# GpSimd begins every second quad of gathers only when the quad before has landed

## The chip, the cores and the metric

The kernel runs on one NeuronCore of a Trainium2 chip, as one program. The metric is the device time of one execution in microseconds (us); lower is better. The engines are TensorE (PE in the profile; PEld is its weight load), VectorE (DVE), ScalarE (ACT), GpSimd (POOL) and SyncE (SP), each with its own instruction stream; they meet at semaphores. All data are fp32.

## What is computed

A block of layers on 6250 nodes with 256 features and 206250 directed edges, sorted by destination. It has three parts; the first is the one that matters here:

```python
src, dst = edge_index
norm = edge_weight * rsqrt(deg_out[src] * deg_in[dst] + EPS)
def _gcn_layer(x, W, b, src, dst, norm, n_nodes):
    xt = x @ W
    msg = xt[src] * norm[:, None]
    agg = segment_sum(msg, dst, num_segments=n_nodes)
    return relu(agg + b)
h6 = _gcn_layer(layernorm(x), W6, b6, ...)
h7 = _gcn_layer(h6, W7, b7, ...)
out = h7 @ Wp + bp
```

A linear attention over the same rows is added to it, and then comes a mixture-of-experts feed-forward layer of which two of eight experts are used, with layer norms. The two graph layers need the feature rows of all source nodes, edge by edge, twice.

## The kernel before

Edges are handled in tiles of 128. The kernel sums over edges first and multiplies by W afterwards. Each of the two graph layers is one **pass** (L = 0 and L = 1 in the code), and in each pass the edge tiles go one of two ways.

Some tiles are *gathered*: GpSimd fetches their 128 source rows from a table in HBM (`t1` in pass 0, 258 floats a row; `t2` in pass 1, 256 floats) by an indirect DMA, one row to a partition (L1960). Four tiles are a **quad** (`QT = 4`), and a quad fills one slot of a ring in SBUF (`msg`, named `ringb` in the profile) that has `RQ = 6` slots. Pass 0 has NQS[0] = 246 quads and pass 1 has 216, so 462 quads and 1848 gathers. Each slot has its own semaphore `s_g[slot]`, to which every gather adds 16 when it has landed, 64 for a quad.

The other tiles are *dense*: for them a block A of adjacency weights (128 destinations by all nodes) is built from one-hot products (L680), and TensorE multiplies it with the feature rows X (L702). In pass 0 the blocks of A are also stored to HBM, and in pass 1 most of them are loaded back by SyncE, in transfers of 1600 KB (L2031 and L2039). Before pass 1 SyncE also reloads X from `t2` in five parts of 1250 KB (L2056).

Both ways are interleaved by hand. TensorE runs through numbered steps. In step s, `sums(L, s)` first does quad s (`mm`, L654 to L665): it waits until the quad has landed (L657) and until its selection matrix `Sb` is ready, multiplies the four tiles, and increments `s_mm`, which frees the ring slot. Then, in the same in-order stream, come the builds, dense products and transposes of that step, and in pass 1 the second layer's row work. VectorE makes `Sb` four quads deep (L1219, L1234); in pass 0 it also reads one column of the gathered rows for that (L1227) and so waits for the landing too.

GpSimd's program (`pool_program`, L1897) does nothing but gathers in the two passes. For quad j it waits, once the ring is full, until TensorE has used the quad six before (L1953), and then issues four gathers (L1958 to L1961). Pass 1 begins when `t2` is stored. After pass 1 the expert layer follows (L873, L886), with 13 small operations of GpSimd (L1965) and no gather. SyncE's loads and stores run on their own queue and share the 16 DMA engines with the gathers.

Of the kernel before, what the change touches and what calls it, by code (L numbers as in the profile page):

```python
# [24 lines left out]
NQ = NG * GR  # L25
# [23 lines left out]
RQ = 6  # L49
# [125 lines left out]
def column(L, j):  # L175

    return GT * SG[L][j // GR] + QT * (j % GR)
# [92 lines left out]
def gnn_block(nc, srcT, srcR, dstT, dstR, dstO, wO, wT, x, W6, b6, W7, b7, Wp, bp, wkvT, woT, wq, bo, lng, lnb,  # L270
              Wr, br, W1, b1, W2, b2, gamma, beta, need, out):
    ctx = ExitStack()
    with ctx:
# [6 lines left out]
        def sem(name):  # L280
            return ctx.enter_context(nc.semaphore(name))
# [171 lines left out]
        s_g = [sem(f"s_g{i}") for i in range(RQ)]  # L453
# [35 lines left out]
        def loads_of(n, parity):  # L489

            return (n + 1 - parity) // 2
# [1405 lines left out]
        def pool_program(e):  # L1897
            e.iota(iof[:, :], [[1, max(HR, P)]], base=0, channel_multiplier=0,
                   allow_small_or_imprecise_dtypes=True).then_inc(s_const, 1)
            e.iota(pidx[:, :], [[0, 1]], base=0, channel_multiplier=1,  # L1900
                   allow_small_or_imprecise_dtypes=True).then_inc(s_const, 1)
            e.memset(ones[:, :], 1.0).then_inc(s_const, 1)
            e.memset(eps5[:, :], 1e-5).then_inc(s_const, 1)
            e.memset(eps12[:, :], 1e-12).then_inc(s_const, 1)
            e.memset(eps30[:, :], 1e-30).then_inc(s_const, 1)
            e.memset(nhalf[:, :], -0.5).then_inc(s_const, 1)
            e.memset(X[:, :, D:XC], 1.0).then_inc(s_const, 1)
            e.wait_ge(l_w, 16)

            def neighbours(n):  # L1910

                m, a_ = divmod(n, 4)
                if n < 0 or m > 3:
                    return
                o, w_ = 512 * a_, 512 + (m in (0, 3) and a_ == 3)
                if n == 0:
                    e.wait_ge(s_dig, 8)
                    e.wait_ge(s_qb, 2)
                if a_ == 0 and m:
                    e.wait_ge(s_pc, n)  # L1920
                if m == 0:
                    e.tensor_tensor(diff[:, o:o + w_], dOf[:, o + 1:o + w_ + 1], dOf[:, o:o + w_], ALU.subtract).then_inc(s_pc, 1)
                if m == 1:
                    e.tensor_tensor(prod[:, o:o + w_], diff[:, o:o + w_], diff[:, o + 1:o + w_ + 1], ALU.mult).then_inc(s_pc, 1)
                if m == 2:
                    e.tensor_tensor(psq[:, o:o + w_], prod[:, o:o + w_], prod[:, o:o + w_], ALU.mult).then_inc(s_pc, 1)
                if m == 3:
                    e.tensor_tensor(pair[:, o:o + w_], wOx[:, o:o + w_], wOx[:, o + 1:o + w_ + 1], ALU.add).then_inc(s_pc, 1)

            for c, (t0, n) in enumerate(BATCHES):  # L1930
                if n > NA:
                    e.wait_ge(s_hh, c + 1)
                    e.tensor_tensor(hot_w[:, c % RD, NA:n, :], hot_hi[:, c % RD, NA:n, :],  # L1933
                                    wn[:, t0 + NA:t0 + n].unsqueeze(2).to_broadcast([P, n - NA, NT]),
                                    ALU.mult).then_inc(s_wp, 1)
                if c % 5 == 0:
                    neighbours(c // 5 - 8)
            for n in range(max((len(BATCHES) - 1) // 5 - 7, 0), 16):
                neighbours(n)

            e.wait_ge(l_t1, 16 * NB)
            e.wait_ge(s_rel, 1)
            e.wait_ge(s_dm, len(BATCHES))
            e.wait_ge(l_dego, 16)
            for L in range(2):
                if L == 1:
                    for k in range(2):
                        e.wait_ge(l_t2[k], 16 * loads_of(NT, k))
                table, width = (t2, D) if L else (t1, TW)
                for j in range(NQS[L]):  # L1950
                    slot = j % RQ
                    if j >= RQ:
                        e.wait_ge(s_mm, L * NQ + j - RQ + 1)  # L1953
                    elif L == 1:
                        e.wait_ge(s_mm, NQ)
                    elif j == 4:
                        e.wait_ge(s_flag, 1)
                    for k in range(QT):  # L1958
                        t = column(L, j) + k
                        e.indirect_dma_start(msg[:, slot * QT + k, 0:width], None, table,  # L1960
                                             bass.IndirectOffsetOnAxis(src[:, t:t + 1], 0)).then_inc(s_g[slot], 16)  # L1961
            for c in range(NC):
                n, k = CHUNKS[c][1], c % 2
                e.wait_ge(f_var, c + 1)
                e.tensor_tensor(rs[0:R, k, 0:n], mv[0:R, k, 0:n, 1], nhalf[0:R, :].to_broadcast([R, n]),  # L1965
                                ALU.pow).then_inc(f_pow, 1)
# [230 lines left out]
        @block.gpsimd  # L2197
        def _(e):
            pool_program(e)
# [56 lines left out]
```

## Time and profile before

| | us |
|---|---|
| median of 3 runs | 3715.28 |
| lowest and highest run | 3714.16, 3717.88 |
| the profiled execution, its own time | 3720.0 |
| its span in the profile | 3718.2 |
| TensorE busy | 3030.2 (81%) |
| GpSimd busy | 2172.4 (58%) |
| VectorE busy | 1803.2 (48%) |
| ScalarE busy | 1150.8 (31%) |

The profile is of one execution. Busy time counts only instructions that work, not waits. For GpSimd a gather's busy time is the making of its descriptors; the data move beside and after it. "Issue" is time in which an engine waited for nothing that the profile shows; "remote" is a wait whose releasing event has no instruction record beside it. Queue q0 carries the gathers, q1 and q10 the transfers issued by the other engines, q8 and q14 the instructions. The granted clock of TensorE is given as a share of full speed.

### The profile page before, as it was taken

The numbers are of one execution on the slowest core, as the hardware profiler recorded it, in microseconds if no ns is written. First come the engines' busy times: TensorE is split into PE (matmuls) and PEld (weight loads), VectorE is DVE, ScalarE is ACT, GpSimd is POOL, SyncE is SP. The second block draws the span as 40 slices with busy tenths as digits, with TensorE's granted clock in tenths as the row PEclk, the third lists the DMA queues.
The fourth block names the chain that finished last, engine by engine and source line by source line (L and its number), as shares of the span: only waits on it lengthen the run. The fifth ranks groups of instructions, "written<-read, shape, count | busy, mean of one in ns | idle before, by whom it ended". The sixth has DMA issues, their size and how long they took to land.

```text
span 3718.2 us, 52328 instructions
## 1 busy us (share of the span) xinstructions
PE 3030.2 (81%) x16152; PEld 2012.8 (54%) x16152; DVE 1803.2 (48%) x4528; ACT 1150.8 (31%) x4063; POOL 2172.4 (58%) x2090
## 2 busy tenths in 40 slices
PE   4777837888888888888885689888888888888998
PEld 3445514555555555555553356556555555555666
DVE  9989835666666666656542133223212324132334
ACT  5787834444444443444330011001000101002211
POOL 4666656666666666666664666666666666630000
PEclk8899967999898998999987789989998998988999
DMA  4331134544544545445456534654655454533221
GB/s 118 99 104 54 56 77 132 159 154 138 172 139 152 161 136 170 139 140 171 129 180 186 131 123 135 204 175 145 197 189 188 152 190 151 191 104 105 78 77 47
DMA packets 219543, 515.58 MB, mean 139 GB/s; under 512 B 62465, under 2 KB 129831, under 8 KB 208169
## 3 DMA queue, kind: packets, MB, share of 16 engines
q0 software_dynamic: 88704, 243.35, 22.8%
q1 hardware_dynamic: 124053, 262.34, 20.8%
q10 hardware_dynamic: 6500, 6.40, 0.6%
q8 instruction: 141, 2.31, 0.3%
q14 instruction: 145, 1.19, 0.1%
HBM read 384.88 MB, written 127.07 MB: 138 GB/s over the span
## 4 chain that ended last, share of the span: by engine, by line
PE 46%; issue 8%; another core or an unknown queue 6%; DVE 3%; DMA 2%; ACT 1%; POOL 1%; DVEq 1%; ACTq 0%; SPq 0%; POOLq 0%
PE ps L702 19%; PE ps L680 7%; PE ps L663 5%; PE ps L873 5%; PE ps L886 4%; PE ps L821 1%; PE ps L824 1%; POOL ringb L1960 1%; PE ps L642 1%; PE ps L809 1%; ACT ab L1737 1%; DMA t<-mbuf 0%; DVE ab L1303 0%; DMA x2d<-accb 0%
## 5 line engine op out<-in xcount | busy, mean ns | idle before, releaser
L1960 POOL DMA_INDIRECT ringb<-t,src x1848 | 1862.5, 1008 | 979.1 <-issue 496.5
L702 PE MATMUL ps<-xb,ab 125*128 125x256 f32 (+1 forms) x4700 | 1253.7, 407 | 83.3 <-issue 80.6
L702 PEld LDWEIGHTS ps<-xb,ab 125*128 125x128 f32 x4700 | 934.9, 203 | 358.5 <-issue 197.7
L680 PE MATMUL ps<-mlb 128*125 128x300 f32 x1260 | 484.1, 475 | 170.4 <-issue 67.9
L1737 ACT ACTIVATE ab<-ps 125x250 f32 x724 | 295.2, 408 | 797.3 <-PE ps L680 408.8
L663 PE MATMUL ps<-ringb,Sb 128*32 128x257 f32 (+1 forms) x3696 | 378.2, 417 | 141.9 <-issue 78.2
L680 PEld LDWEIGHTS ps<-mlb 128*125 128x125 f32 x1260 | 228.1, 205 | 335.7 <-issue 298.1
L1933 POOL TENSOR_TENSOR ab<-ab,wn 128x100 f32<-128x100 f32 x201 | 274.6, 1371 | 167.7 <-DVE ab L1086 167.7
L604 PE MATMUL ps<-ab 128*50 128x125 f32 x3228 | 222.7, 286 | 132.3 <-ACT ab L1659 45.0
L1270 DVE TENSOR_TENSOR mlb<-iof,rel 128x900 f32<-128x900 f32 (+1 forms) x231 | 232.2, 1005 | 172.5 <-remote 104.6
L1659 ACT ACTIVATE ab<-ab,wn 128x50 f32<-128x50 f32 x1212 | 288.8, 330 | 18.6 <-DVE ab L1086 18.6
L604 PEld LDWEIGHTS ps<-ab 128*50 128x50 f32 x3228 | 181.9, 131 | 196.4 <-issue 100.3
L663 PEld LDWEIGHTS ps<-ringb,Sb 128*32 128x32 f32 x3696 | 90.5, 111 | 362.3 <-issue 290.3
L1219 DVE TENSOR_TENSOR Sb<-iof,rel 128x128 f32<-128x128 f32 x462 | 131.2, 284 | 315.6 <-remote 156.5
L1250 DVE TENSOR_TENSOR accb<-accb,ps 128x96 f32 (+1 forms) x308 | 73.7, 239 | 410.9 <-remote 315.4
L1303 DVE TENSOR_TENSOR ab<-ab,side 125x50 f32 x724 | 177.7, 245 | 165.5 <-DVE ab L1303 74.8
L1088 DVE TENSOR_TENSOR ab<-iof,ringb 128x1000 f32<-128x1000 f32 x202 | 248.9, 1232 | 0.0
L1965 POOL TENSOR_TENSOR rs<-mv,consts 125x4 f32<-125x4 f32 (+1 forms) x13 | 12.8, 988 | 391.6 <-DVE mv L1606 391.6
L1751 ACT ACTIVATE mlb<-mlb,wn 128x125 f32<-128x125 f32 x630 | 208.2, 395 | 91.7 <-issue 47.7
L873 PE MATMUL ps<-xb 128*128 128x500 f32 (+1 forms) x416 | 172.3, 573 | 4.3 <-DMA Sb<-in_b 3.8
L886 PE MATMUL ps<-xb,ab 128*125 128x256 f32 x800 | 174.6, 379 | 0.0
L886 PEld LDWEIGHTS ps<-xb,ab 128*125 128x125 f32 x800 | 150.1, 188 | 27.0 <-issue 5.1
(245 smaller groups left out, 2704.3 us busy)
## 6 DMA issues: line engine op xcount, KB each, us to landing
ad<-ab SPq DMA_DIRECT2D x42, 1600.0 KB
ab<-ad SPq DMA_DIRECT2D x42, 1600.0 KB
ringb<-t,src POOLq DMA_INDIRECT x1848
kvd<-mlb SPq DMA_DIRECT2D x50, 256.0 KB, 2.1
kvb<-kvd SPq DMA_DIRECT2D x50, 256.0 KB
x2t<-mlb SPq DMA_DIRECT2D x13, 500.0 KB
xb<-x2t SPq DMA_DIRECT2D x13, 500.0 KB, 8.2
xb<-in_x SPq DMA_DIRECT2D x10, 625.0 KB
```

What stands on the lines that cost most here:

```text
L604: ins = e.matmul(PS[j % 2][o:o + NT, 0:R], hot_w[:, r, j, :], hot_lo[:, r, j, :], start=t0 + j < 2, stop=t0 + j >= T - 2)
L663: ins = e.matmul(PS[g % 2][k * W:(k + 1) * W, 0:wd], Sb[:, qi % NS, k, :], msg[:, slot * QT + k, 0:wd], start=r == 0, stop=r == GR - 1)
L680: e.matmul(PS[bank_of(t)][0:R, 0:HR], low[:, slot_of(t), :], high[:, slot_of(t), :], start=True, stop=True).then_inc(s_bld, 1)
L702: ins = e.matmul(PS[dense_bank(L, d)][:, 0:wd], lhs, X[0:R, k, 0:wd], start=k == 0, stop=k == NT - 1)
L873: ins = e.matmul(PS[j][:, 0:wd], M1[:, k, h, j * P:(j + 1) * P], XF[c % RF][:, h, 0:wd], start=h == 0, stop=h == 1)
L886: ins = e.matmul(pb[0:R, t * D:(t + 1) * D], hT[:, rr, m, (t0 + t) * R:(t0 + t + 1) * R], M2[:, m // 4, m % 4, :], start=m == 0, stop=m == 7)
L1088: e.tensor_tensor(hot_lo[:, r, 0:n, :], iof[:, 0:R].unsqueeze(1).to_broadcast([P, n, R]), lo_f[:, t0:t0 + n].unsqueeze(2).to_broadcast([P, ...
L1270: e.tensor_tensor(Mb[:, o:o + n, :], iof[:, 0:HR].unsqueeze(1).to_broadcast([P, n, HR]), rel[:, c0:c0 + n].unsqueeze(2).to_broadcast([P, n ...
L1659: e.activation(hot_w[:, r, j, :], hot_hi[:, r, j, :], ACT.Copy, scale=wn[:, t0 + j:t0 + j + 1]).then_inc(s_wa, 1)
L1737: e.activation(A1[place][:, :, bass.ds(b, RT - 1)], bank[:, :, 1:RT], ACT.Copy).then_inc(s_ev, 1)
L1933: e.tensor_tensor(hot_w[:, c % RD, NA:n, :], hot_hi[:, c % RD, NA:n, :], wn[:, t0 + NA:t0 + n].unsqueeze(2).to_broadcast([P, n - NA, NT]), ...
L1960: e.indirect_dma_start(msg[:, slot * QT + k, 0:width], None, table, bass.IndirectOffsetOnAxis(src[:, t:t + 1], 0)).then_inc(s_g[slot], 16)
```

## The change

Three lines are added to GpSimd's loop over the quads. At every even j from 2 on, in both passes, GpSimd waits, before it issues the first gather of quad j, until `s_g` of the slot of quad j - 1 has the count that it reaches when that quad's four gathers have all landed. So quads 0 and 1 are issued together, then 2 and 3 when 1 has landed, and so on. The wait for a free slot stays as it is, and nothing else is changed.

```diff
                         e.wait_ge(s_mm, NQ)
                     elif j == 4:
                         e.wait_ge(s_flag, 1)
+                    if j >= 1 and j % 2 == 0:
+                        landed = (j - 1) % RQ
+                        e.wait_ge(s_g[landed], 64 * (L * len(range(landed, NQ, RQ)) + (j - 1) // RQ + 1))
                     for k in range(QT):
                         t = column(L, j) + k
                         e.indirect_dma_start(msg[:, slot * QT + k, 0:width], None, table,
```

## Rows read from the trace of the kernel before

**Rows 1.** The page, sections 1, 4 and 5: busy time, chain, costly groups.

```profile
PE 3030.2 (81%) x16152; PEld 2012.8 (54%) x16152; DVE 1803.2 (48%) x4528; ACT 1150.8 (31%) x4063; POOL 2172.4 (58%) x2090
...
PE ps L702 19%; PE ps L680 7%; PE ps L663 5%; PE ps L873 5%; PE ps L886 4%; PE ps L821 1%; PE ps L824 1%; POOL ringb L1960 1%; PE ps L642 1%; PE ps L809 1%; ACT ab L1737 1%; DMA t<-mbuf 0%; DVE ab L1303 0%; DMA x2d<-accb 0%
...
L702 PE MATMUL ps<-xb,ab 125*128 125x256 f32 (+1 forms) x4700 | 1253.7, 407 | 83.3 <-issue 80.6
```

**Rows 2.** Windows: length, busy PE PEld DVE ACT POOL; clock, DMA share, GB/s.

```profile
492.00:1996.00 1504.00, 1225.88 (x6058) 807.51 (x6062) 872.60 (x2408) 594.05 (x2175) 1026.05 (x984) 0.90 0.48 150
2026.00:3307.00 1281.00, 1076.93 (x5162) 717.74 (x5163) 347.12 (x1144) 122.53 (x373) 836.44 (x864) 0.88 0.52 164
3307.00:3718.00 411.00, 373.68 (x1362) 250.42 (x1360) 143.62 (x329) 79.38 (x130) 12.85 (x14) 0.96 0.25 80
```

**Rows 3.** GpSimd in pass 0: waits (us, times, longest); its group, with releasers.

```profile
POOL ringb L1960 <- issue: 261.6, 858, 0.3
...
L1960 POOL DMA_INDIRECT ringb<-t,src x984 | 1026.1, 1043 | 498.4 <-issue 261.6 <-remote 162.1 <-PE ps L663 48.1
```

**Rows 4.** The same for GpSimd in pass 1.

```profile
POOL ringb L1960 <- issue: 234.9, 766, 1.0
...
L1960 POOL DMA_INDIRECT ringb<-t,src x864 | 836.4, 968 | 480.7 <-issue 234.9 <-remote 144.6 <-PE ps L663 64.3
```

**Rows 5.** Waits for landings of gathers, 492 to 3307 us.

```profile
PEld ps L663 <- DMA ringb<-t,src: 67.3, 8, 25.1
...
PE ps L663 <- DMA ringb<-t,src: 34.0, 5, 18.2
...
DVE wn L1227 <- DMA ringb<-t,src: 25.1, 9, 6.0
```

**Rows 6.** Timeline, start of pass 0: start us, us, instruction, idle before.

```profile
496.91 0.95 POOL L1960 DMA_INDIRECT ringb<-t,src  x1 [0.30 <-issue]
...
499.72 0.17 DVE L1227 TENSOR_TENSOR wn<-wn,ringb 128x4 f32<-128x4 f32 x1 [6.02 <-DMA ringb<-t,src]
...
501.93 0.95 POOL L1960 DMA_INDIRECT ringb<-t,src  x1 [0.30 <-issue]
...
504.76 0.17 DVE L1227 TENSOR_TENSOR wn<-wn,ringb 128x4 f32<-128x4 f32 x1 [4.34 <-DMA ringb<-t,src]
```

**Rows 7.** Timeline, start of pass 1.

```profile
2026.24 10.44 SPq L2056 DMA_DIRECT2D xb<-t  x2
...
2030.56 0.95 POOL L1960 DMA_INDIRECT ringb<-t,src  x1 [0.30 <-issue]
...
2036.83 1.08 PE L663 MATMUL ps<-ringb,Sb 128*32 128x256 f32 x8 [18.16 <-DMA ringb<-t,src]
...
2045.73 0.95 POOL L1960 DMA_INDIRECT ringb<-t,src  x1 [0.30 <-issue]
...
2051.87 1.08 PE L663 MATMUL ps<-ringb,Sb 128*32 128x256 f32 x8 [4.08 <-DMA ringb<-t,src]
```

**Rows 8.** DMA queues: packets, MB, share; pass 0, then pass 1.

```profile
q0 software_dynamic: 47232, 130.05, 30.9%
q1 hardware_dynamic: 17076, 88.49, 15.8%
q10 hardware_dynamic: 6110, 6.02, 1.3%
...
q0 software_dynamic: 41415, 113.17, 29.9%
q1 hardware_dynamic: 35798, 96.08, 21.9%
```

**Rows 9.** DMA queues, 2100 to 2130 us.

```profile
q0 software_dynamic: 997, 2.69, 31.2%
q1 hardware_dynamic: 3, 0.01, 0.1%
```

**Rows 10.** A window of 2 us during a load of A.

```profile
2458.00:2460.00 2.00, 2.00 (x8) 1.14 (x7) 0.00 (x0) 0.00 (x0) 1.70 (x2) 1.00 1.03 417
```

## The prediction

> **What bounds the kernel now.** I read the page first. TensorE is busy 81% of the span and its matmuls lead the chain that ended last, line by line; GpSimd is busy 58%, and its gathers (L1960) hold only 1% of that chain [rows 1]. So the work that the change touches is off the path today. The question is how far off, so next come the two stretches in which gathers run: pass 0 from 492 to 1996 us and pass 1 from 2026 to 3307 us. TensorE is busy 1225.88 of 1504 us in the first and 1076.93 of 1281 us in the second [rows 2]: TensorE and what it waits for set the pace. The last 411 us [rows 2] hold no gather and can't change.
>
> Then GpSimd's own books in each pass. Pass 0: 984 gathers of 1043 ns, 261.6 us between them under "issue", and 162.1 + 48.1 = 210.2 us of waiting for a ring slot. "remote" is counted with "PE ps L663", because the only wait that this engine's code has there is the one on `s_mm` [rows 3]. Pass 1: 864 gathers of 968 ns, 234.9 us of issue, 144.6 + 64.3 = 208.9 us of waiting for a slot [rows 4]. These two sums, 210 and 209 us, are all the slack that GpSimd has; what the change adds beyond them comes out at the end. From the other side: TensorE and VectorE waited for a gather's landing only 8 + 5 + 9 times in both passes together [rows 5]. The ring of six quads is nearly always full, and the landings are hidden.
>
> **What the change adds.** From quad 2 on, each even quad waits until the quad before it has landed. In pass 0 that is j = 2 to 244, 122 waits; in pass 1, j = 2 to 214, 107 waits; 229 in all. It removes and moves nothing. Queued behind the waiting instruction are only later gathers, since GpSimd does nothing else in these passes. When it passes, no gather is in flight. Who waits for that, once the ring has run dry: TensorE's L663, its next instruction in program order, with all the dense products behind it; in pass 0 VectorE's L1227 too. SyncE's queue isn't held.
>
> Call G the time from the end of a quad's fourth gather to the start of the next gather, where the new wait ends last. The trace has no such wait on GpSimd, so I bound G by engines that did wait for a landing. With little else moving (start of pass 0), the fourth gathers end at 496.91 + 0.95 = 497.86 and 501.93 + 0.95 = 502.88 us, and VectorE's L1227 starts at 499.72 and 504.76: 1.86 and 1.88 us [rows 6]. With two reloads of 1250 KB on SyncE's queue (start of pass 1), TensorE waits so for four quads in a row. For the first and the last of them the fourth gathers end at 2030.56 + 0.95 = 2031.51 and 2045.73 + 0.95 = 2046.68 us, and TensorE starts at 2036.83 and 2051.87: 5.32 and 5.19 us [rows 7]. So G is 1.87 us when the gathers are alone and about 5.25 us under bulk traffic.
>
> How often is there bulk traffic? In pass 0 the gather queue q0 takes 30.9% of the DMA engines' time, the others 15.8 + 1.3 = 17.1% [rows 8]. In a stretch with gathers alone q0 takes 31.2% [rows 9], and under a load of A the engines are full, 1.03 [rows 10]. So others fill what q0 leaves in about 17.1 / (100 - 30.9) = 0.25 of pass 0. In pass 1 it is 21.9 / (100 - 29.9) = 0.31 [rows 8]. Mixed G: 1.87 + 0.25 x 3.38 = 2.72 us in pass 0, and 1.87 + 0.31 x 3.38 = 2.92 us in pass 1. These are estimates from the rows named.
>
> **The sum.** GpSimd's new length of pass 0 is 1026.1 of gathers, 861 short gaps of 0.305 us (261.6 / 858), so 262.6, and 122 G. The old one is 1026.1 + 261.6 + 210.2. The difference is 122 G - 209 = 332 - 209 = +123 us. Pass 1: 836.4 + 756 x 0.307 = 232.1 + 107 G against 836.4 + 234.9 + 208.9, so 107 G - 212 = 312 - 212 = +100 us. Together +223 us. This takes for granted that the slot waits vanish altogether: with an average quad of 5.40 + (2.72 - 0.31) / 2 = 6.6 us on GpSimd against 1498 / 246 = 6.1 us at which TensorE now uses them, the ring runs dry early and stays so. GpSimd becomes the bound, and TensorE's own stalls are absorbed in it. Filling the ring hides only the first few pairs: it is three pairs deep, under 3 x 1 us.
>
> The whole is linear in G: 229 G - 421. The point of balance is G = 1.84 us, about the quiet value itself. Ends: with 1.87 everywhere +7 us, with 5.25 everywhere +781 us. I take the mix because both kinds of traffic are in the trace in known shares. Two things may lower it: the last gather of a pair no longer has its successors beside it, and a longer pass holds the same bulk bytes, so fewer pairs meet them. If the bulk excess falls by a quarter, G is 2.51 and 2.66, +170 us. One thing may raise it: GpSimd may take some 0.2 us longer to start after a landing than the engines in [rows 6, 7], 229 x 0.2 = +46 us. These nearly cancel, so I stay at the sum, rounded to +225.
>
> Against the profiled run, span 3718.2 and own time 3720.0, that is 3945; the median of the three runs is 3715.3, 5 us less, so I predict 3940 us.
>
> **Rule and trace.** A gather lands 1.87 or 5.25 us after its issue, by what else is moving [rows 6, 7]. The Trainium skill ("DMA: Bandwidth & Descriptors", section "Queues, rings and completion order") says that each DMA engine takes turns between its queues, a whole packet at a time; that fits, and speaks for a wait whose price depends on the neighbours. The same page of the Trainium skill, section "Anatomy of one DMA", speaks against the forecast: it gives one DMA about 2.0 us plus its bytes over 436 GB/s, so an estimate by that page of 2.3 us for the 132 KB of a gather, from its start; less the 0.95 us of issue that would be G = 1.35, and no loss. The trace has 2.81 us from start to consumer (496.91 to 499.72 [rows 6]) even when quiet, so it doesn't agree.
>
> **The rivals.**
> *The landing stays hidden.* If the landing came within a fixed time of under 1.84 us after issue whatever else moves, the new wait would only take the place of the slot waits that GpSimd already has (210 and 209 us [rows 3, 4]), and the time would stay at 3715, at most 3722. The quiet rows stand at this edge; the bulk rows speak against it. 5%. The code leaves no way for the waits to be empty: the awaited count is the one that L657 awaits for the same quad, and just-issued gathers can't have reached it.
> *Faster.* Gathers in bursts leave the DMA engines to the reloads of A, and TensorE, which now bounds, meets fewer late operands. Its place is the dense product L702, whose idle time before it is 83.3 us in MATMUL records [rows 1]; a fifth of that gone is -17 us, 3698. It needs G under 1.84, because otherwise GpSimd bounds. Since gathers alone take only 31% of the engines, little is freed. 2%.
> *The pairs under bulk traffic cost more than the mix says.* If the busy share of pairs is nearer to a half (the transfers are not at full rate all the time, so they last longer than their share says), G is 3.56 us, 229 x 3.56 - 421 = +394 us, 4110. And TensorE idling in each pair may lower its granted clock further (0.90 and 0.88 now [rows 2]). 13%.
> *As forecast,* G between 2.3 and 3.3 us, +106 to +335: 80%.
>
> **How the numbers follow.** Forecast 3940 us. The range leaves out the hidden and the faster case (7%) and most of the costly one: from G = 2.35 (+117) to G = 3.3 (+335), rounded to 3825 to 4050. A difference of 0.2%, 7 us, is about the least that a measurement of this kernel can tell. Faster by over 0.2%: 0.02; within: 0.05; slower: 0.93.
>
> **What the profile after should show.** GpSimd: no waits for PE L663 or remote on `s_mm` beyond a handful; instead about 229 waits for its own gathers, mean G near 2.8 us, in two clusters near 1.9 and 5. Gathers still near 1.0 us each. Pass 0 some 120 us longer, pass 1 some 100 us, the last 411 us unchanged. TensorE and VectorE waiting often for `ringb`; TensorE's busy share down to 76 or 77%. The forecast is wrong if slot waits remain in number (TensorE still bounds), if G is one narrow cluster, or if TensorE's busy time itself grows.

## The result

The changed kernel takes 4174.4 us (median of 4 runs, 4166.0 to 4180.0) against 3716.6 us (3714.2 to 3720.2): 1.123 times, with a 95% interval of 1.1216 to 1.1246. It is slower by 458 us, twice the 225 us forecast and outside the range. The profiled execution took 4174.9 us, its span is 4173.1.

The page of the changed kernel: busy times, the chain that ended last by engine and by line, and two groups. L1963 is the gather (L1960 before).

```profile
PE 3065.2 (73%) x16152; PEld 2069.1 (50%) x16152; DVE 1808.2 (43%) x4528; ACT 1151.1 (28%) x4063; POOL 2172.9 (52%) x2090
...
POOL 33%; DMA 23%; PE 21%; issue 15%; DVE 7%; ACT 1%; DVEq 0%; another core or an unknown queue 0%; POOLq 0%; ACTq 0%; SPq 0%
POOL ringb L1963 32%; DMA ringb<-t,src 21%; PE ps L873 4%; PE ps L886 4%; PE ps L702 3%; DVE ab L1088 3%; PE ps L680 2%; PE ps L604 2%; PE ps L663 2%; PE ps L592 1%; DVE ab L1086 1%; POOL ab L1933 1%; DMA xtd<-mlb 1%; PE ps L642 1%; ACT ab L1659 0%
...
L1963 POOL DMA_INDIRECT ringb<-t,src x1848 | 1861.7, 1007 | 1444.9 <-DMA ringb<-t,src 631.8
...
L663 PE MATMUL ps<-ringb,Sb 128*32 128x257 f32 (+1 forms) x3696 | 345.3, 447 | 487.7 <-DMA ringb<-t,src 419.1
```

In place of TensorE, GpSimd's gathers (32%) and their DMAs (21%) now lead the chain; before, L1960 held 1% [rows 1]. TensorE is busy 73% of the span instead of 81%.

Windows of the changed kernel: pass 0, pass 1 and the tail, with the columns of [rows 2].

```profile
490.00:2218.00 1728.00, 1265.68 (x6040) 842.84 (x6040) 875.08 (x2401) 596.70 (x2174) 1029.74 (x984) 0.85 0.43 133
2244.00:3772.00 1528.00, 1080.19 (x5221) 744.70 (x5219) 353.65 (x1162) 124.46 (x380) 831.93 (x864) 0.85 0.44 139
3772.00:4173.00 401.00, 367.21 (x1312) 245.84 (x1312) 140.70 (x319) 78.30 (x127) 12.85 (x13) 0.95 0.24 77
```

The passes are longer and the tail is not. From the first gather's start to the last one's end, pass 0 went from 1497.9 to 1726.8 us (+229) and pass 1 from 1280.2 to 1526.1 (+246). Between the passes it fell from 37.0 to 27.1 us and after them from 411 to 402, together -19. That is the whole difference of the spans, 455 us. TensorE's busy time rose by only 35 us, at a granted clock of 0.85 instead of 0.90 and 0.88.

GpSimd's gathers in pass 0 and in pass 1 of the changed kernel: busy us, mean ns, idle before them and what ended it, which answers to [rows 3, 4].

```profile
L1963 POOL DMA_INDIRECT ringb<-t,src x984 | 1029.7, 1046 | 723.6 <-DMA ringb<-t,src 320.3 <-issue 308.9 <-PE ps L663 65.3
...
L1963 POOL DMA_INDIRECT ringb<-t,src x864 | 831.9, 963 | 721.3 <-DMA ringb<-t,src 311.5 <-issue 246.9 <-PE ps L663 133.2
```

These rows give G, the time from a quad's last gather to the next where the new wait stands. Pass 0: 723.6, less 26.5 for the first gather's wait, less 861 short gaps of 0.305 us, is 434.5 us for 122 waits: G = 3.56. Pass 1: 721.3 - 27.1 - 756 x 0.305 = 463.6 us for 107 waits: G = 4.33. The forecast had 2.72 and 2.92. Put into its own sum, 122 x 3.56 - 209 + 107 x 4.33 - 212 = +477 us, against 475 measured in the two passes. That the two agree to 2 us is close to arithmetic, since a pass is GpSimd's gathers and the gaps between them; what it tells is that the gathers kept their length and that no slot wait stands beside the new ones. The size of G was wrong.

Waits for landings in both passes, to be read beside [rows 5].

```profile
DVE wn L1227 <- DMA ringb<-t,src: 635.4, 204, 13.8
POOL ringb L1963 <- DMA ringb<-t,src: 631.8, 156, 9.2
...
PEld ps L663 <- DMA ringb<-t,src: 545.4, 156, 24.1
PE ps L663 <- DMA ringb<-t,src: 416.9, 129, 12.2
```

VectorE waits 204 times, TensorE 156 times; before it was 9 and 8. The profile puts some of GpSimd's new waits under "issue" and "PE ps L663" too, so its row for the gathers' DMA, 156, undercounts the 229.

### The profile page after: what moved, and what is told of

Read it like the earlier page. It is cut to its first block, busy times and chain, and to the rows that moved or that the text cites. A ratio compares the mean times of both kernels' runs of the same rounds, so it can differ in the third digit from the quotient of the medians.

```text
span 4173.1 us, 52556 instructions
## 1 busy us (share of the span) xinstructions
PE 3065.2 (73%) x16152; PEld 2069.1 (50%) x16152; DVE 1808.2 (43%) x4528; ACT 1151.1 (28%) x4063; POOL 2172.9 (52%) x2090
## 4 chain that ended last, share of the span: by engine, by line
POOL 33%; DMA 23%; PE 21%; issue 15%; DVE 7%; ACT 1%; DVEq 0%; another core or an unknown queue 0%; POOLq 0%; ACTq 0%; SPq 0%
POOL ringb L1963 32%; DMA ringb<-t,src 21%; PE ps L873 4%; PE ps L886 4%; PE ps L702 3%; DVE ab L1088 3%; PE ps L680 2%; PE ps L604 2%; PE ps L663 2%; PE ps L592 1%; DVE ab L1086 1%; POOL ab L1933 1%; DMA xtd<-mlb 1%; PE ps L642 1%; ACT ab L1659 0%
## 5 line engine op out<-in xcount | busy, mean ns | idle before, releaser
L1963 POOL DMA_INDIRECT ringb<-t,src x1848 | 1861.7, 1007 | 1444.9 <-DMA ringb<-t,src 631.8
L702 PE MATMUL ps<-xb,ab 125*128 125x256 f32 (+1 forms) x4700 | 1292.2, 421 | 21.3 <-issue 15.7
L702 PEld LDWEIGHTS ps<-xb,ab 125*128 125x128 f32 x4700 | 981.2, 213 | 308.8 <-issue 126.4
L663 PE MATMUL ps<-ringb,Sb 128*32 128x257 f32 (+1 forms) x3696 | 345.3, 447 | 487.7 <-DMA ringb<-t,src 419.1
L680 PE MATMUL ps<-mlb 128*125 128x300 f32 x1260 | 496.2, 489 | 137.7 <-ACT side L1741 53.4
L663 PEld LDWEIGHTS ps<-ringb,Sb 128*32 128x32 f32 x3696 | 79.1, 115 | 677.9 <-DMA ringb<-t,src 548.0
L680 PEld LDWEIGHTS ps<-mlb 128*125 128x125 f32 x1260 | 241.2, 213 | 296.3 <-issue 259.4
L1227 DVE TENSOR_TENSOR wn<-wn,ringb 128x4 f32<-128x4 f32 x246 | 40.5, 165 | 661.6 <-DMA ringb<-t,src 635.4
L604 PE MATMUL ps<-ab 128*50 128x125 f32 x3228 | 221.3, 285 | 132.2 <-ACT ab L1659 44.6
L604 PEld LDWEIGHTS ps<-ab 128*50 128x50 f32 x3228 | 180.9, 131 | 196.5 <-issue 98.9
L873 PE MATMUL ps<-xb 128*128 128x500 f32 (+1 forms) x416 | 171.9, 571 | 4.1 <-DMA Sb<-in_b 3.6
```

The lines of the kernel that those rows point to most:

```text
L604: ins = e.matmul(PS[j % 2][o:o + NT, 0:R], hot_w[:, r, j, :], hot_lo[:, r, j, :], start=t0 + j < 2, stop=t0 + j >= T - 2)
L663: ins = e.matmul(PS[g % 2][k * W:(k + 1) * W, 0:wd], Sb[:, qi % NS, k, :], msg[:, slot * QT + k, 0:wd], start=r == 0, stop=r == GR - 1)
L680: e.matmul(PS[bank_of(t)][0:R, 0:HR], low[:, slot_of(t), :], high[:, slot_of(t), :], start=True, stop=True).then_inc(s_bld, 1)
L702: ins = e.matmul(PS[dense_bank(L, d)][:, 0:wd], lhs, X[0:R, k, 0:wd], start=k == 0, stop=k == NT - 1)
L873: ins = e.matmul(PS[j][:, 0:wd], M1[:, k, h, j * P:(j + 1) * P], XF[c % RF][:, h, 0:wd], start=h == 0, stop=h == 1)
```

## Experiments

Runs sent together ran on one chip, beside the kernel before. That kernel took 3716.6 (A, with the result above), 3714.8 (B), 3686.7 (C), 3367.8 (D) and 3715.3 us (E). B to E are four different chips; which one A is was not recorded, and it may be one of them. D stands apart, and this matters below. The changed kernel itself ran on A and E alone. Where chips differ, lengths of passes are compared, taken as above.

**Waiting for an older quad (chip B).**

```diff
-                    if j >= 1 and j % 2 == 0:
-                        landed = (j - 1) % RQ
-                        e.wait_ge(s_g[landed], 64 * (... + (j - 1) // RQ + 1))
+                    if j >= 4 and j % 2 == 0:
+                        landed = (j - 4) % RQ
+                        e.wait_ge(s_g[landed], 64 * (... + (j - 4) // RQ + 1))
```

> The same number of added waits, at the same places, but each for quad j - 4 (from j = 4), whose gathers were issued some 15 us before. Theory 1 (the loss is the time from the last gather's issue to its landing, plus the start after it): these waits are met when reached, so at most the gap before the even quad grows from 0.30 us to under 0.8 us, 227 x 0.5 = 113 us, which the slot waits (419 us in the kernel before) swallow: 3716 us, within 8. Theory 2 (a second wait costs by itself, whatever it waits for, and lands on the path): 3716 + 113 = 3830 us.

Measured: 3714.6 us, 0.9999 of before (0.9990 to 1.0009). A wait that is met when GpSimd comes to it costs nothing that shows here. Slack could hide a small cost, but the trace has none: 118 of the 227 gaps with such a wait are 0.305 us, as short as any gap. The loss lies in what is waited for.

**The two waits swapped (chip B).**

```diff
+                    if j >= 1 and j % 2 == 0:
+                        landed = (j - 1) % RQ
+                        e.wait_ge(s_g[landed], ...)
                     if j >= RQ:
                         e.wait_ge(s_mm, L * NQ + j - RQ + 1)
...
-                    if j >= 1 and j % 2 == 0:
-                        landed = (j - 1) % RQ
-                        e.wait_ge(s_g[landed], ...)
```

> The changed kernel with the order of its two waits swapped: the landing first, the free slot second, so that the gather's own instruction may carry the wait for the landing. Theory 1 (the changed kernel's GpSimd starts 0.77 us after a landing because the wait for it is an instruction of its own, against 0.26 us where the gather itself carries the wait): 0.5 us less at each of 229 waits, -115 us, 4060 us. Theory 2 (0.77 us is how long GpSimd takes to see a DMA's semaphore, in whatever form it waits): 4174 us, within 10.

Measured: 4051.2 us, 1.0900 (1.0881 to 1.0920), 123 us less than the changed kernel. The timeline of GpSimd in the changed kernel, quads 2, 4, 6 and 8, with the idle time before each in brackets:

```profile
503.12 0.95 POOL L1963 DMA_INDIRECT ringb<-t,src  x1 [2.08 <-DMA ringb<-t,src]
...
515.78 1.26 POOL L1963 DMA_INDIRECT ringb<-t,src  x1 [2.59 <-DMA ringb<-t,src]
...
528.43 0.94 POOL L1963 DMA_INDIRECT ringb<-t,src  x1 [2.62 <-DMA ringb<-t,src]
...
541.97 0.94 POOL L1963 DMA_INDIRECT ringb<-t,src  x1 [2.58 <-DMA ringb<-t,src]
```

and quads 2, 4 and 6 with the waits swapped:

```profile
503.16 0.94 POOL L1963 DMA_INDIRECT ringb<-t,src  x1 [2.16 <-DMA ringb<-t,src]
...
515.28 0.94 POOL L1963 DMA_INDIRECT ringb<-t,src  x1 [2.08 <-DMA ringb<-t,src]
...
527.10 0.94 POOL L1963 DMA_INDIRECT ringb<-t,src  x1 [2.09 <-DMA ringb<-t,src]
```

Quad 2 waits for the landing alone (the ring is not yet full), and its gap is 2.08 us. From quad 4 on a second wait stands beside it, and the gap is 2.6 us. Swapped, all are near 2.1. The instruction records of the two traces show what differs: of two waits, the one written first stands on the gather itself, the other becomes a semaphore instruction of its own (17 ns) ahead of it. In the changed kernel that instruction waits for the landing, and the gather starts 0.765 us after the landing in 201 of 229 cases. With the waits swapped the gather itself holds the wait for the landing, and it starts 0.26 us after it in 204 cases. So 0.5 us of nearly each of 229 gaps comes from the order in which two waits are written. Why a wait of its own costs that much is not shown.

About every ninth wait takes 0.95 us more again. Its row, quad 14, at a place where little else moves (the gap is 3.56 us instead of 2.6):

```profile
577.65 1.68 POOL L1963 DMA_INDIRECT ringb<-t,src  x1 [0.30 <-issue]
582.89 1.00 POOL L1963 DMA_INDIRECT ringb<-t,src  x1 [3.56 <-issue]
```

It happens at quads 14, 32, 50, 68 and so on, every 18th, in both passes, with 1.71 us from landing to start. With the waits swapped the same 25 quads take 0.92 us. Its cause was not tried; it adds about 25 us in all. The two differences, 204 x 0.5 and 25 x 0.79 us, make the 123 us of the swap.

**Pass 0 alone (chip B).**

```diff
-                    if j >= 1 and j % 2 == 0:
+                    if L == 0 and j >= 1 and j % 2 == 0:
```

> The change in pass 0 alone (122 of its 229 waits). Theory 1 (each pass pays for its own waits, nothing carries over): pass 0 longer by 229 us as in the changed kernel, the stretch to pass 1 shorter by 10, pass 1 as before, 3716 + 219 = 3935 us. Theory 2 (the loss of pass 1 is partly what a late pass 0 leaves, in transfers or in TensorE's clock): pass 1 grows too, by tens of us, and the time is above 3960 us.

Measured: 3935.3 us, 1.0599 (1.0582 to 1.0617). Pass 0 is 1726.8 us long, as in the changed kernel to a tenth; pass 1 1274.6, 6 us under the kernel before. Nothing carries over.

**One or two more gathers under way (chips B and C).** The wait moves behind the first gather of the even quad or, with k == 2 in place of k == 1, behind the second.

```diff
                     for k in range(QT):
+                        if k == 1 and j >= 1 and j % 2 == 0:
+                            landed = (j - 1) % RQ
+                            e.wait_ge(s_g[landed], ...)
                         t = column(L, j) + k
```

> The changed kernel, with the wait moved behind the first gather of the even quad, so that one more gather is under way while GpSimd waits. Theory 1 (the sum of the gaps on GpSimd is the loss, slope 1): each wait is shorter by one gather and its gap, 1.25 us, so mean G falls from 3.95 to about 2.7 and the time by 229 x 1.25 = 286 us, to 3890 us; a little less gain, some 3910 us, if the landing in quiet stretches is nearly covered. Theory 2 (what costs is that the gathers come in bursts and that each wait for a whole quad lets other transfers get ahead): the time stays within 80 us of the changed kernel's 4174 us.

Measured: 3896.2 us, 1.0494 (1.0473 to 1.0515). 278 of the expected 286 us came back.

> The changed kernel, with the wait behind the second gather of the even quad. Theory 1 (sum of gaps, with a floor where the landing is covered): each wait is 2.5 us shorter, but no gap falls below 0.3 to 0.5 us. About half the gaps are near 2.6 us and vanish, the others keep some 3 us: mean near 1.7, under the balance of 1.84, 229 x 1.7 - 421 < 0, so TensorE bounds again, with some tens of us where stretches of bulk traffic outrun the ring: 3740 us, 3716 to 3770. Theory 2 (a fixed cost per wait however long it is): more than 3800 us.

Measured: 3798.9 us, 1.0324 (1.0300 to 1.0348), +112 us over before on this chip, where +24 was expected. GpSimd's waits in this run:

```profile
POOL ringb L1963 <- issue: 496.5, 1620, 1.1
...
POOL ringb L1963 <- DMA ringb<-t,src: 215.8, 62, 7.7
POOL ringb L1963 <- remote: 205.4, 100, 5.5
...
POOL ringb L1963 <- PE ps L663: 98.1, 64, 6.0
```

By the sum of gaps this kernel should have tied. It didn't, because the slot waits did not vanish: 205.4 us of "remote" and 98.1 of "PE ps L663" stand beside 215.8 us of landings. In quiet stretches the ring fills and GpSimd waits for TensorE; in bulk traffic it waits for landings and the ring runs dry. Pass 0 is 1513.7 us (+16 against chip A), pass 1 1352.9 (+73). So slack in one stretch did not pay for a wait in another; that the six quads of the ring set how far it reaches is argued, not shown.

**Bulk traffic taken away (chip C).** The stores and reloads of A move 128 of 3200 columns.

```diff
-                e.dma_start(ad[d][:, p * SW:(p + 1) * SW], ab[:, o:o + SW])...
+                e.dma_start(ad[d][:, p * SW:p * SW + CUT], ab[:, o:o + CUT])...
...
-                    e.dma_start(ab[:, k * AP_ + q * SW:k * AP_ + (q + 1) * SW],
-                                ad[d][:, q * SW:(q + 1) * SW])...
+                    e.dma_start(ab[:, k * AP_ + q * SW:k * AP_ + q * SW + CUT],
+                                ad[d][:, q * SW:q * SW + CUT])...
```

> The kernel before, with the stores and reloads of A (84 transfers of 1600 KB) cut to their first 128 of 3200 columns, 64 KB each; pass 1 then multiplies with stale blocks, so this leaves work out: only traffic is taken away. Theory 1 (bulk traffic is hidden in the kernel before): 3716 us or up to 40 us less, where reloads had held TensorE. Theory 2 (these transfers slow the kernel in other ways): over 100 us less. It is the yardstick for the next run.

> The changed kernel with the same transfers of A cut (work is left out in the same way). Theory 1 (in bulk traffic the landing takes 5 us and more, and that makes about half of the loss): mean G falls from 3.56 and 4.33 us to about 2.65 in pass 0 and 2.9 in pass 1, where smaller transfers remain; 122 x 2.65 + 107 x 2.9 - 421 = +213 us over the kernel before with the same cut. Theory 2 (long landings come from the gathers themselves, their rows scattered in HBM): the loss stays near +458 us over it.

Measured: 3677.0 us without the waits, 0.9975 of before (0.9959 to 0.9990), and 4012.8 us with them, 1.0897 (1.0877 to 1.0917). The loss over the kernel with the same cut is 336 us, between the two expectations. GpSimd's gathers in pass 0 of the changed kernel with the cut:

```profile
L1964 POOL DMA_INDIRECT ringb<-t,src x984 | 1027.8, 1044 | 633.6 <-issue 299.6 <-DMA ringb<-t,src 249.3 <-PE ps L664 58.1
```

633.6 - 26.6 - 262.6 = 344.4 us for 122 waits: G = 2.82 in place of 3.56. In pass 1 G is only down from 4.33 to 3.71, and other transfers of 250 to 500 KB (rows of x, x2 and their transposes) remain there. Counting landings of odd quads that come over 3 us after issue, the cut took them from 29 to 5 of 123 in pass 0, and from 41 to 34 of 108 in pass 1. The DMA records tie both kinds to the traffic. In the changed kernel queues other than q0 had 0.74 (pass 0) and 0.45 (pass 1) of the engines' time in the 1.7 us after the issue of a quad that landed late, and 0.01 and 0.03 after the others. With the cut, pass 1 has 0.27 for its 34 late ones and under 0.01 for the rest.

How a single long gap looks in the uncut changed kernel: first two windows of 4 us (columns as in [rows 2]), then the gaps that follow them, then the DMA queues of the second one, 2549 to 2557 us.

```profile
2519.00:2523.00 4.00, 4.00 (x25) 2.90 (x24) 0.42 (x1) 0.00 (x0) 1.47 (x2) 1.00 0.32 93
2550.00:2554.00 4.00, 0.19 (x1) 0.00 (x0) 0.00 (x0) 0.00 (x0) 0.00 (x0) 1.00 1.00 421
```

```profile
2523.25 1.04 POOL L1963 DMA_INDIRECT ringb<-t,src  x1 [2.48 <-PE ps L663]
...
2557.61 0.95 POOL L1963 DMA_INDIRECT ringb<-t,src  x1 [8.10 <-DMA ringb<-t,src]
```

```profile
q1 hardware_dynamic: 213, 2.32, 69.0%
q0 software_dynamic: 192, 0.52, 16.5%
```

With the engines at 0.32, gathers alone, the gap is 2.48 us. With a load of A, when they stand at 1.00 and 421 GB/s and that load has 69.0% of their time, it is 8.10 us, and TensorE is busy 0.19 of 4 us meanwhile. The Trainium skill ("DMA: Bandwidth & Descriptors", section "Queues, rings and completion order") has each DMA engine take turns between queues at whole packets, and this trace agrees with it in kind: q0 keeps 16.5% of the engines, a gather still gets through, only late. How much goes in one turn it does not show.

**Both together (chip D).** The swapped waits and the cut transfers in one kernel, its diff the sum of both.

> Swapped waits and cut transfers of A together (work is left out as in the other run with cut transfers). Theory 1 (the start after a landing and the traffic of A are two separate terms of the same gap): the loss of the changed kernel with cut transfers, 336 us, less what the swap brought by itself, 123 us: +213 us over the kernel before with the same cut, 1.055 to 1.06 times the kernel before. Theory 2 (both act on the same waits and overlap): clearly above, over 1.07.

Measured: 3887.8 us, 1.1549 (1.1530 to 1.1568) of the 3367.8 us that the kernel before takes there. The ratio is spoilt by the chip, the lengths are not: pass 0 1550.6 and pass 1 1410.6 us, against 1634.7 and 1461.1 with the cut alone. That is 135 us less; the swap alone had brought 76 + 46 = 121. The two terms add. (Against the 3677.0 us of the kernel with the cut on chip C it is +211 us, where +213 was expected.)

**A wait at every quad (chip D).**

```diff
-                    if j >= 1 and j % 2 == 0:
+                    if j >= 1:
```

> The change with a wait at every quad instead of every second one: 460 waits instead of 229. Theory 1 (loss = sum of gaps minus the slack, and the 419 us of slack can be used up only once): with mean gaps a little under those of the changed kernel, 3.45 and 4.1 us, 245 x (3.45 - 0.31) - 210 = +559 in pass 0 and 215 x (4.1 - 0.31) - 209 = +606 in pass 1, together +1165 us, 4880 us: two and a half times the loss for twice the waits. Theory 2 (each wait costs a fixed 2 us by itself): twice the loss, +916 us, 4632 us.

Measured: 4820.2 us, 1.4312 (1.4288 to 1.4336) of before there, and 1104 us over chip A's. Twice the waits cost 2.4 times the loss.

```profile
POOL ringb L1963 <- DMA ringb<-t,src: 1044.1, 283, 9.7
POOL ringb L1963 <- issue: 520.4, 1412, 6.7
POOL ringb L1963 <- PE ps L663: 462.4, 151, 9.4
```

The three rows are 2026.9 us of idle time in 1846 gaps; less 1846 x 0.305 = 563 us for the shortest gap that there is, the excess is 1464 us. Against the kernel before on the same chip the loss is 4820.2 - 3367.8 = 1452 us, nearly all of it. The kernel before has 496.5 + 306.7 + 112.4 - 563 = 353 us of excess on chip A (GpSimd's waits, each the sum of both passes' rows: 261.6 + 234.9, 162.1 + 144.6, 48.1 + 64.3 [rows 3, 4]). 1464 - 353 = +1111 us.

**A shallower ring (chips C and D).** At most four quads in the ring, in the changed kernel and in the kernel before.

```diff
-                    if j >= RQ:
-                        e.wait_ge(s_mm, L * NQ + j - RQ + 1)
+                    if j >= 4:
+                        e.wait_ge(s_mm, L * NQ + j - 4 + 1)
...
-                    elif j == 4:
+                    if j == 4 and L == 0:
                         e.wait_ge(s_flag, 1)
```

> The changed kernel, with the wait for a free slot tightened so that at most four quads are in the ring instead of six. Theory 1 (GpSimd bounds both passes, the ring is nearly empty and its depth is not used): at most 20 us more, 4174 to 4195 us. Theory 2 (TensorE still bounds in stretches, and the 57 waits for TensorE that the profile of the changed kernel shows on GpSimd are real): over 60 us more, above 4235 us.

Measured: 4170.4 us, 1.1329 (1.1299 to 1.1358) of before there. Passes of 1730.8 and 1520.6 us, where the changed kernel has 1726.8 and 1526.1. The depth of the ring is unused, so the rows that blame TensorE for some of GpSimd's waits name the wrong one of two waits. The records of the changed kernel agree: in all 228 cases with two waits the semaphore instruction that waits for the landing ends 0.04 us after it, and the gather follows.

> The kernel before with at most four quads in the ring. In the changed kernel the same tightening left both passes as they were. Theory 1 (in the kernel before TensorE bounds and gathers run ahead in the ring, four quads of some 6 us each still covering nearly every landing): 15 to 60 us more, since less is stored for stretches of bulk traffic. Theory 2 (GpSimd is already close to bounding, so any tightening shows): over 100 us more.

Measured: 3393.3 us, 1.0081 (1.0064 to 1.0098), +25 us. Its profile is the one look at a kernel without the new wait on chip D. GpSimd's waits there:

```profile
POOL ringb L1960 <- issue: 552.6, 1814, 0.3
...
POOL ringb L1960 <- PE ps L663: 38.0, 32, 6.8
```

There are no slot waits to speak of (38 us), where chip A had 419: on this chip GpSimd already issues without pause, even with the shallower ring. The kernel before is faster on D by 3716.6 - 3367.8 = 349 us, close to the 353 us of excess that GpSimd has on A.

**Waiting two quads back (chip D).**

```diff
-                    if j >= 1 and j % 2 == 0:
-                        landed = (j - 1) % RQ
+                    if j >= 2 and j % 2 == 0:
+                        landed = (j - 2) % RQ
```

> The wait at every even quad j, but for quad j - 2 instead of j - 1, so that four gathers (5.0 us of issue) are still under way. Theory 1 (what counts is how much of the landing time is not covered, stretch by stretch): quiet landings are covered, only the longest in bulk traffic are not, mostly in pass 1: 10 to 50 us more, 3726 to 3766 us. Theory 2 (a barrier on GpSimd costs whenever it isn't met at once and draining is what hurts): over 3800 us.

Measured: 3475.9 us, 1.0334 (1.0309 to 1.0359), +108 us, over the expected 10 to 50. GpSimd's waits:

```profile
POOL ringb L1963 <- issue: 531.8, 1737, 1.4
...
POOL ringb L1963 <- PE ps L663: 71.9, 50, 7.2
POOL ringb L1963 <- DMA ringb<-t,src: 69.9, 59, 3.7
```

531.8 + 71.9 + 69.9 = 673.6 us, less 563, is 111 us of excess: on this chip nothing swallows it, and the loss is the excess to a few us. Chip A's slack would have taken part of it; that was not run there.

**TensorE made lighter (chip E).** 20 of each 50 matmuls of the dense products are left out.

```diff
+                if k % 2 and k % 10 != 9:
+                    return
                 ins = e.matmul(PS[dense_bank(L, d)][:, 0:wd], lhs, X[0:R, k, 0:wd], ...)
```

> The kernel before with 20 of each 50 matmuls of the dense products left out (the odd steps but each tenth), so it leaves work out. Theory 1 (in the kernel before TensorE sets the pace and GpSimd's 419 us of slot waits are only TensorE's lateness): with TensorE lighter, GpSimd's own issue bounds both passes, and the time falls by 350 to 419 us, to 3300 to 3370 us, where the kernel before takes 3687 or 3716 us; on a chip where it takes 3368 us, by at most 60 us. Theory 2 (other things than TensorE's load, chains over VectorE and ScalarE, set the pace): less than 150 us.

> The changed kernel with the same matmuls left out. Theory 1 (its two passes last as long as GpSimd's gathers and gaps, whatever TensorE does): within 25 us of the changed kernel, 4150 to 4200 us, on any chip. Theory 2 (TensorE's work is part of its path): at least 60 us less.

> The changed kernel itself, beside the light pair. Theory 1 (a kernel bound by GpSimd takes the same on every chip): 4165 to 4185 us, whatever the kernel before takes there. Theory 2 (the change costs a fixed ratio of 1.12): 1.12 times the kernel before on this chip.

Measured: without the waits 3700.3 us, 0.9957 of before (0.9943 to 0.9970); with them 4155.5 us, 1.1182 (1.1162 to 1.1203); the changed kernel itself 4172.6 us, 1.1224 (1.1201 to 1.1247). The changed kernel does not care how much TensorE has to do (-17 us). But the kernel before doesn't either (-15 us, where 350 to 419 were expected), and that goes against theory 1. The page of the light kernel without waits (busy times and the dense product), then its waits:

```profile
PE 2733.2 (74%) x14272; PEld 1691.9 (46%) x14272; DVE 1800.8 (49%) x4528; ACT 1148.1 (31%) x4063; POOL 2176.6 (59%) x2090
...
L704 PE MATMUL ps<-xb,ab 125*128 125x256 f32 (+1 forms) x2820 | 866.1, 431 | 112.0 <-issue 104.3
```

```profile
POOL ringb L1962 <- issue: 507.4, 1662, 0.7
PEld ps L680 <- issue: 479.2, 371, 12.9
...
POOL ringb L1962 <- remote: 286.2, 133, 6.4
```

TensorE's busy time fell by 297 us, where two fifths of the dense products' 1253.7 us [rows 1] would be 501: the matmuls that are left took longer (431 ns in place of 407), at a granted clock of 0.85 instead of 0.90. What it waits for without a visible reason rose. "PEld ps L680 <- issue" was 317.9 us in the kernel before (chip A):

```profile
PEld ps L680 <- issue: 317.9, 339, 10.8
```

and on chip D, in the kernel with four quads in the ring:

```profile
PEld ps L680 <- issue: 149.3, 268, 5.8
```

So on A and E something holds TensorE back, whatever its load, and on D much less. The semaphore records of the traces say where. GpSimd's slot waits end when a quad's last matmul (L663) increments `s_mm`. On D that comes within 0.3 us of the end that the profile models for this matmul, in 461 of 462 cases. In the kernel before on A it comes a median of 2.0 us later, and over 1 us later in 278 of the 443 increments on record. On B (the wait for an older quad), C (the cut transfers, without waits) and E (the light kernel, without waits) it is over 1 us in 293 of 438, 290 of 441 and 300 of 436. The builds (L680) and dense products do the same; the matmuls before and after the passes (L604, L873) don't, on any chip. So on the slower chips TensorE ends its work in the passes later than its rows in the profile show, and "remote" in GpSimd's rows is that lateness: a release with no matmul record beside it. This is where the slack comes from that the forecast counted on. Why TensorE is late there, and not on D, stays open.

## Why the prediction was wrong

*TensorE bounds before, GpSimd after.* Right where GpSimd had slack: the chain, the unused ring and the light kernel with its waits show it. That TensorE's load was the bound before is not right: with 40% fewer dense matmuls the time stayed within 0.4%, though the rest ran at a lower clock. GpSimd waited for matmuls that ended late.

*Only the waits matter, nothing is moved.* Right: waits met at once cost nothing that shows, the passes are independent, and the tail is no longer than before. TensorE's busy time did grow, which the forecast had named as a sign of being wrong, but by 35 us and off the path.

*The sum 122 G - 209 and 107 G - 212.* Right: with the measured G it gives 477 for 475 us. The slot waits did vanish, as it took for granted.

*G in quiet stretches, 1.87 us.* This step failed. It was read from VectorE's L1227, which waits for this one semaphore and holds the wait itself, and GpSimd had two waits, of which that for the landing became an instruction of its own. Measured: 2.6 us in the quiet rows, 0.73 us over [rows 6]. The swap took back 0.5 of them; the rest is the "some 0.2 us" for a slower start of GpSimd that the forecast named and then let cancel. With the 25 quads that take 0.95 us more it makes 229 x 0.73 + 25 = about 190 us, three quarters of the miss of 252 us (477 - 225).

*The share of bulk traffic, 0.25 and 0.31, and its 5.25 us.* In pass 0, 29 of 123 landings took over 3 us (0.24), as forecast. In pass 1 it was 41 of 108 (0.38), and these took 5.95 us on average, plus 0.77 to the next start, against the 5.25 us in all taken from [rows 7]. The share could have been counted ahead: in the kernel before 44 of 108 landings of odd quads in pass 1 took over 3 us (0.41), and 26 of 121 in pass 0 (0.21). In pass 1 the gaps hold 107 x (4.33 - 2.60 - 0.11 - 1.05) = 61 us more for bulk traffic than forecast. That is the other quarter. What A's traffic has in the gaps is what the cut took out of them, 122 x (3.56 - 2.82) + 107 x (4.33 - 3.71) = 157 us. The loss fell by less, 458 - 336 = 122 us, but that compares chip A with chip C. On C alone it fell by 484 - 336 = 148 us, if the changed kernel with four quads in the ring (4170.4 us) stands for the uncut one.

*A quarter less bulk excess, because bursts relieve the queues.* Not seen: landings in pass 1 came 3.46 us after the issue on average in the changed kernel, 3.23 before.

*The rival in which landings stay hidden, and the estimate of 1.35 us.* Refuted. The shortest of all 229 gaps is 2.08 us, over the 1.84 us of balance. *The rival with costlier pairs* (+394 us, 13%) came nearest, and the loss was larger still. Its reason, that nearer to half of the pairs meet bulk traffic, holds in part for pass 1 (0.38) and not for pass 0 (0.24); that pass 0 has just its G of 3.56 us is chance. *The faster rival*: with bulk traffic away, the kernel before gained 0.25%, so little was to be had.

*The range* took its ends from G = 2.35 to 3.3. The mean over both passes is 3.92, since the quiet value alone is 2.6 before any bulk traffic is added: a start after a landing that the trace of before showed on no GpSimd row.

## What to carry to other kernels

Price a new wait as its gap on the waiting engine, times the number of waits, minus the slack that this engine has in the same stretch; read the gap from that engine's own waits and with all the waits that stand there, not from another engine. Of two waits before one instruction of GpSimd, try the one that is met last in first place, so that the instruction itself holds it: in this kernel that order alone is worth 3%. And slack that comes from another engine's lateness may not be there on the next chip: the kernel before had 419 us of it on A, and the four-quad one 38 us on D.

## What the runs showed that was not expected

The start after a met wait is 0.26 us on GpSimd when the gather carries it and 0.765 us when a semaphore instruction ahead of it does. Every 18th quad took 1.71 us (0.92 with the waits swapped). The kernel before takes 3368 us on one chip and 3687 to 3717 us elsewhere, while the changed kernel took 4174.4 and 4172.6 us on A and E, and pass lengths on D agreed with sums from A. On all chips but D TensorE's matmuls in the passes end up to several us after their modelled ends. And leaving out 1880 of TensorE's 4700 dense matmul records changed the time by 0.4%.
